# A causal mask copied into three score buffers by ScalarE, and a new order of maxima and feed-forward tiles, in a decoder layer

## The reference

```python
x = x + self_attention(layernorm(x))       # 16 query heads, 4 key heads of 16, latent projections, rotary, causal
x = x + cross_attention(layernorm(x), ctx) # 16 heads of 16, int mask shared by all batches and heads
x = x + ffn(layernorm(x))                  # 256 -> 1024 relu -> 256, hidden values and w2 rounded to 4-bit-exponent fp8

# both attentions
scores = q @ k.T * 16 ** -0.5
scores = where(masked, -inf or -1e9, scores)
out = softmax(scores) @ v
```

## Time and profile before

| what | value |
|---|---|
| median of 3 runs | 1891.46 us (1891.41 to 1894.48) |
| the profiled execution, its own time | 1879.75 us |
| its span, first to last instruction | 1878.1 us |
| mean granted TensorE clock | 0.962 |
| busy share of the span: TensorE / weight loads | 90% / 54% |
| busy share: VectorE / ScalarE / GpSimd | 66% / 59% / 37% |

### The profile page before, as it was taken

How to read it: one execution, slowest core, us unless ns; L and a number is a source line. 1 busy time by engine, 2 the same in 40 slices (tenths; PEclk the granted TensorE clock), 3 DMA queues, 4 the chain that set the end, 5 groups by cost and what they waited for, 6 DMA issues and landing times.

```text
span 1878.1 us, 34264 instructions
## 1 busy us (share of the span) xinstructions
PE 1683.7 (90%) x12302; PEld 1017.6 (54%) x12302; DVE 1242.5 (66%) x1908; ACT 1110.7 (59%) x1720; POOL 701.0 (37%) x962
## 2 busy tenths in 40 slices
PE   2879989899998989999899999989999898999887
PEld 1445555556554655655556554655655555565554
DVE  4467576676857667575776857668585766857562
ACT  3355665756567465656756566475656746565563
POOL 3260533625144261533526153262524426152300
PEclk7879999999999999999999998999999999999999
DMA  6351632725254270633626163271625427063310
GB/s 173 51 89 26 94 66 37 121 26 86 47 80 78 35 124 8 87 64 52 106 35 94 31 93 65 35 124 20 89 50 74 84 35 111 18 88 55 51 31 12
DMA packets 86607, 124.09 MB, mean 66 GB/s; under 512 B 10481, under 2 KB 53938, under 8 KB 86322
## 3 DMA queue, kind: packets, MB, share of 16 engines
q1 hardware_dynamic: 83650, 115.26, 40.5%
q0 software_dynamic: 2160, 7.87, 1.1%
q10 hardware_dynamic: 768, 0.57, 0.1%
HBM read 21.42 MB, written 8.39 MB: 16 GB/s over the span
## 4 chain that ended last, share of the span: by engine, by line
PE 62%; POOL 9%; issue 9%; ACT 7%; DMA 7%; DVE 6%; SPq 1%; POOLq 0%; ACTq 0%
PE o_pair L1312 12%; PE small L1398 7%; PE score L1273 6%; PE small L1429 5%; PE small L1143 4%; DMA Q<-q2p 3%; PE small L1325 3%; DVE negmax L894 3%; PE score L1250 3%; DMA Q<-negT 2%; PE score L1231 2%; PE score L1196 2%; PE small L1159 2%; POOL x L494 2%; POOL q1f L518 2%
## 5 line engine op out<-in xcount | busy, mean ns | idle before, releaser
L689 ACT ACTIVATE P<-score 128x1024 f32<-128x1024 f32 x448 | 448.4, 1025 | 145.5 <-PE score L1250 56.6
L894 DVE TENSOR_REDUCE negmax<-score 128x4 f32<-128x1024 f32 (+1 forms) x384 | 463.3, 1221 | 66.4 <-PE score L1231 49.9
L916 DVE TENSOR_TENSOR P<-P,cross_bound 128x1024 f32<-128x1024 f32 x192 | 251.0, 1330 | 118.1 <-ACT P L689 118.1
L1312 PE MATMUL o_pair<-P,V 128*32 128x256 f32 (+1 forms) x4096 | 293.8, 374 | 0.3 <-DVE P L916 0.3
L465 POOL TENSOR_TENSOR negrest<-negmax,negparts 128x32 f32<-128x32 f32 x64 | 15.9, 248 | 629.9 <-ACT negparts L650 629.5
L735 ACT ACTIVATE score<-cross_q 128x1024 f32<-128x1024 bf16 x192 | 194.9, 1021 | 31.8 <-DVE negmax L894 31.1
L1429 PE MATMUL small<-xnT,w 128*128 128x256 f32 x720 | 185.2, 379 | 0.0
L1273 PE MATMUL score<-Q,K 99*128 99x256 bf16 x1024 | 168.1, 291 | 8.2 <-ACT P L689 4.3
L1312 PEld LDWEIGHTS o_pair<-P,V 128*32 128x32 f32 x4096 | 87.3, 109 | 142.7 <-issue 86.7
L1231 PE MATMUL score<-K,Q 96*128 96x256 bf16 x768 | 119.3, 279 | 40.1 <-ACT score L735 19.7
L1273 PEld LDWEIGHTS score<-Q,K 99*128 99x128 bf16 x1024 | 87.4, 102 | 112.4 <-issue 63.6
(11 more groups left out here) (181 smaller groups left out, 3142.1 us busy)
## 6 DMA issues: line engine op xcount, KB each, us to landing
Q<-q1p SPq DMA_DIRECT2D x96, 256.0 KB, 5.9
K<-k2p SPq DMA_DIRECT2D x96, 256.0 KB, 8.3
Q<-q2p SPq DMA_DIRECT2D x192, 128.0 KB, 4.5
x_in<-in_x SPq DMA_DIRECT2D x16, 512.0 KB, 5.6
ctxT<-in_ctx SPq DMA_DIRECT2D x16, 512.0 KB, 6.3
k2f<-q1f SPq DMA_DIRECT2D x32, 256.0 KB, 4.9
out_y<-x POOLq DMA_DIRECT2D x15, 512.0 KB, 6.1
K<-k1p SPq DMA_DIRECT2D x96, 64.0 KB, 4.5
```

The source lines that it names most:

```text
L689: A.activation(P[:, t % 4, :], score[b][:, :, :], ACT.Exp, scale=SCALE).then_inc(score_free[b], 1)
L894: V.tensor_reduce(negmax[:, k, h:h + 1024 // w], s.rearrange("p (h w) -> p h w", w=w), AX.X, ALU.max, negate=True).then_inc(score_free[b], 1)
L916: V.tensor_tensor(p, p, cross_bound[:, t % 2, :].unsqueeze(1).broadcast_to([128, 4, SEQ]), ALU.min).then_inc(probs_masked[1], 1)
L1312: last = T.matmul(o_ps[ob][32 * j:32 * j + 32, SEQ * gg + q0:SEQ * gg + SEQ], v, p, start=s == 0, stop=end, tile_position=(0, 32 * j), ski ...
```

## The change

The self score tiles 3 to 11 get their causal mask from ScalarE (`self_premask`), as the cross tiles do, and no longer from TensorE; the self tiles use three buffers, with `o_pair` as the third, instead of two. Cross tile 8 is masked by TensorE instead of ScalarE. The cuts of the maxima are moved: GpSimd cuts the second cross half ahead of `add_ffn`, and the second self half is cut by ScalarE and GpSimd ahead of the exponentials instead of between them; `turn_max` moves from after tile 2 to after tile 1 (self) and tile 3 (cross). `add_bias2` moves to the next body. `h1` and `h2` go into the middle, ahead of and behind the transposes `xnT2_1`, the quarters of `h3` to `h7` are spread by `PIECES`, and VectorE makes the third part of the first cross query half before it applies the norm. `v2_0` is computed on both sides of self tile 2, and banks are given out in the new order.

```diff
 def body_users
-    attention = (["k2_0"] + p("m2T_1", "o2t0", "o2t1", "o2t2", "o2t3")
-                 + ["v2_0", "k2_1", "m1T_0"] + p("oT2_0", "oT2_1") + p("out2_0", "out2_1")
+    attention = (["k2_0"] + p("m2T_1", "o2t0", "o2t1", "o2t2") + ["v2_0"] + p("o2t3")
+                 + ["k2_1", "m1T_0"] + p("oT2_0", "oT2_1") + p("out2_0", "out2_1")
...
-              + ["xnT2_1"] + p("h1") + ["q2_1"])
-    scores = p("h2", "h3", "h4", "h5", "h6", "h7") + ["m2T_0"] + p("ffn0", "ffn1")
+              + p("h1") + ["xnT2_1"] + p("h2") + ["q2_1"])
+    scores = p("h3", "h4", "h5", "h6", "h7") + ["m2T_0"] + p("ffn0", "ffn1")
...
-        PE_MASKED = (2,)
+        PE_MASKED = (2, 8)
+        SELF_PE_MASKED = 3
+        PIECES = (2, 2, 1, 2, 2, 2, 2, 2, 1, 2, 2, 0)
+        EVICT_AFTER = (4, 6, 8, 11, 12)
...
 gpsimd, add_bias1
+                    pool.wait_ge(part3["q2"], GB * (g - 1) + 1)
 gpsimd, body
-                if prev:
-                    cut_rest(1, i - 1, 1)
-                    cut_third(1, i - 1, 1)
                 cut_rest(0, i, 0)
                 cut_third(0, i, 0)
                 if nxt:
                     inverse_root(0, i + 1)
+                if prev:
+                    add_bias2(i - 1)
                 cut_rest(0, i, 1)
+                cut_third(0, i, 1)
                 for t in range(N1):
...
-                    if t == 0:
-                        cut_third(0, i, 1)
...
-                add_bias2(i)
...
                     third("k1", i + 1)
+                cut_rest(1, i, 1)
+                cut_third(1, i, 1)
                 if prev:
                     add_ffn(st, i - 1)
 scalar, exponentials
-                    if t == 0:
+                    if t == 0 and a == 1:
                         cut_second(a, g, 1)
...
-                    if t == 2:
+                    if t == (1, 3)[a]:
                         maxima(st, a, 1)
 scalar
+            def self_premask(g, t):
+                n, before = self_tile(g, t)
+                act.wait_ge(score_free[n], before)
+                if t % 6 < 4:
+                    A.activation(bufs[n][:, :, :].rearrange("p c (j k) -> p (c j) k", j=2),
+                                 causal_q[:, :].unsqueeze(1).broadcast_to([128, 4, SEQ]),
+                                 ACT.Copy).then_inc(masked[n], 1)
...
 scalar, body
+                for t in range(3, 7):
+                    self_premask(i, t)
+                keys_second(st, 0)
+                self_premask(i, 7)
+                self_premask(i, 8)
                 cut_first(0, i, 0)
+                self_premask(i, 9)
                 cut_second(0, i, 0)
                 keys(st, 1)
-                keys_second(st, 0)
+                self_premask(i, 10)
                 maxima(st, 0, 0)
+                self_premask(i, 11)
+                keys_second(st, 1)
                 if prev:
                     turns(st, "oT2_", inT)
-                keys_second(st, 1)
                 cut_first(0, i, 1)
+                cut_second(0, i, 1)
                 exponentials(st, 0, i)
...
                 premask(i, 0)
+                if prev:
+                    hidden(st, [1])
                 turn_batch(st, "xnT2_1", 1, inT)
                 premask(i, 1)
                 if prev:
-                    hidden(st, [1])
+                    hidden(st, [2])
 vector, body
                 query2_rest(st, i, 0)
+                query2_third(i, 0)
                 norm_apply(1, x2, GB * i + 1, range(2, 4))
-                query2_third(i, 0)
                 query2_rest(st, i, 1)
 tensor, self_scores
+                    if not by_pe:
+                        pe.wait_ge(masked[n], use + 1)
+                    elif n == 2:
+                        for ob in range(2):
+                            if positive(g * UNITS):
+                                pe.wait_ge(o_free[ob], g * UNITS)
...
-                        for c in range(2):
-                            last = T.matmul(score[n][:, c, :], identb[:, :],
-                                            again(causal_q, 4), start=False, stop=True,
-                                            skip_group_check=True)
 tensor, attend
-                    if t == 2:
+                    if t == (1, 3)[a]:
                         turn_max(st, a, g, 1)
 tensor, body
                 if prev:
                     attend(st, 1, i - 1, "scores")
+                    tokens(st, "v2", ctxT, wv2, 0, 0)
...
+                tokens(st, "v2", ctxT, wv2, 0, 1)
                 self_scores(i, [3])
...
-                tokens(st, "v2", ctxT, wv2, 0, 0)
                 self_scores(i, [5])
-                tokens(st, "v2", ctxT, wv2, 0, 1)
                 self_scores(i, [6])
                 key2(st, 1, 0)
...
+                if prev:
+                    hidden(st, [1])
                 pe.wait_ge(xn_ready[1], GB * i + 2)
                 turned_batch(st, "xnT2_1", 1, xn)
                 if prev:
-                    hidden(st, [1])
+                    hidden(st, [2])
```

More of the change, by code:

```diff
@@ L303, in tile, with self_tile, cross_tile, masked_told @@
             return n % 2, g * (TILES // 2) + n // 2
-        def cross_use(g, t):
+        def self_tile(g, t):
+            n = t % 3
+            return n, g * (TILES // 2 if n < 2 else SELF_USES + CROSS_USES[2]) + t // 3
+        def cross_tile(g, t):
             n = CROSS_BUF[t]
-            return n, g * CROSS_USES[n] + CROSS_BUF[:t].count(n)
-        def cross_tile(g, t):
-            n, use = cross_use(g, t)
-            return (n, use) if n == 2 else (n, g * (TILES // 2) + N1 + CROSS_BUF[:t].count(n))
-        def cross_masked(g, t):
-            n = CROSS_BUF[t]
-            told = [u for u in range(N2) if u not in PE_MASKED and CROSS_BUF[u] == n]
-            return n, g * len(told) + told.index(t)
+            use = CROSS_BUF[:t].count(n)
+            return (n, g * (SELF_USES + CROSS_USES[2]) + SELF_USES + use) if n == 2 else \
+                (n, g * (TILES // 2) + SELF_USES + N1 // 2 + use)
+        def masked_told(n):
+            return ([("S1", t) for t in range(SELF_PE_MASKED, N1) if t % 3 == n]
+                    + [("S2", t) for t in range(N2) if t not in PE_MASKED and CROSS_BUF[t] == n])
+        def masked_use(phase, g, t):
+            n = t % 3 if phase == "S1" else CROSS_BUF[t]
+            told = masked_told(n)
+            return n, g * len(told) + told.index((phase, t))
         def last_cross_tiles(b):
@@ L600, in _ @@
             body(NG - 1, True, False)
-            cut_rest(1, NG - 1, 1)
-            cut_third(1, NG - 1, 1)
+            add_bias2(NG - 1)
             inverse_root(2, NG - 1)
@@ L645, in cut_first @@
                 last = N1 // GB * (b + 1) - 1
-                for t in (last, last - 1) if a == 0 else last_cross_tiles(b):
-                    n, before = tile("S1", g, t) if a == 0 else cross_tile(g, t)
+                for t in (last, last - 1, last - 2) if a == 0 else last_cross_tiles(b):
+                    n, before = self_tile(g, t) if a == 0 else cross_tile(g, t)
                     act.wait_ge(score_free[n], before + 1)
@@ L820, in body @@
                 for t in range(3, N2):
-                    premask(i, t)
-                    if prev and t in (3, 4, 6, 8, 10, 12):
-                        hidden(st, [max(t // 2 + 1, 2 + (t > 3))])
+                    if t not in PE_MASKED:
+                        premask(i, t)
+                    if prev and t in EVICT_AFTER:
+                        hidden(st, [3 + EVICT_AFTER.index(t)])
                     if t == 10:
@@ L1190, in self_scores @@
                     b, s = t // 6, t % 6
-                    n, before = tile("S1", g, t)
-                    if positive(before):
+                    n, before = self_tile(g, t)
+                    by_pe = t < SELF_PE_MASKED
+                    if not by_pe:
+                        _, use = masked_use("S1", g, t)
+                        pe.wait_ge(masked[n], use + 1)
[3 more added lines that the diff above has]
+                                pe.wait_ge(o_free[ob], g * UNITS)
+                    elif positive(before):
                         pe.wait_ge(score_free[n], before)
@@ L1219, in cross_scores @@
                     b = k // 2
-                    n, use = cross_masked(g, t) if t not in PE_MASKED else cross_tile(g, t)
+                    n, use = masked_use("S2", g, t) if t not in PE_MASKED else cross_tile(g, t)
                     if t not in PE_MASKED:
@@ L1560, in body @@
                     if prev and t < 12:
-                        for n in (2 * t, 2 * t + 1):
-                            hidden_part(st, 2 + n // 4, n % 4)
+                        for n in range(sum(PIECES[:t]), sum(PIECES[:t + 1])):
+                            hidden_part(st, 3 + n // 4, n % 4)
                     elif prev:
```

56 lines of the change are left out of this document (33 added, 23 removed).

## The result

The kernel became slower: 1922.12 us as the median of four runs (1911.23 to 1933.39), against 1891.43 for the kernel before. The ratio is 1.0174 with a 95% interval of 1.0130 to 1.0218. The forecast of 1821 us and its range, 1778 to 1864, both missed, and on the wrong side.

A forecast was written before the change was run, and what follows sets the result against it. TensorE was taken to be near its bound (busy 103.5 of about 111.5 us an iteration). Terms -3.0 + 2.2 - 0.9 - 2.0 - 0.7 = -4.4 us, times 16 is -70, from 1891.5 to 1821 us; range 1778 to 1864.

The forecast's parts named there:

- head of the cross part: Start of the cross probabilities: cuts ahead of `add_ffn` remove TensorE's 2.60 us wait; -3.0 us an iteration.
- Self maxima: Self maxima stage: VectorE sets it, so moving masks off TensorE buys almost nothing and new waits cost +2.2 us.
- (c): Self maxima: `k2_1` waits for VectorE to read `v2_0` after maximum 5; TensorE stands from +5.7 to +7.95 before `key2`.
- (d): Self maxima: turns of `oT2` queue on ScalarE behind tile 11's copy and `keys_second`; `out2` starts at 15.75, against 13.6.
- (b): Self maxima: the loop of ScalarE copy, tile and maximum takes 2.9 against VectorE's 3.6 us, so at no cost.
- Self probabilities: Self probabilities: earlier cuts and no 0.58 us DMA wait; tile 6 starts at 6.8 instead of 7.75; -0.9 us.
- Middle and cross maxima: Middle and cross maxima: `h2` moves ahead of the cross scores, cross maxima take 23.2 against 25.5 us; -2.0 together.
- Clock: Whole iteration: the 2.60 us gap and its clock fall go, new gaps come; half of today's 1.4, -0.7 us.
- C: Rival, chance 0.09: clock falls in the self maxima, 13.6 us at half clock an iteration; 1919 us.
- A: Rival, chance 0.12: copies and the bank of `k2_1` cost nothing, VectorE has no gap, clock stays up; 1768 us.
- B: Rival, chance 0.20: the head's wait moves; cross tile 8 waits for its maxima in the DMA queue; 1845 us.
- D: Rival, chance 0.05: no change; self maxima lose all the rest gains, +6.6 instead of +2.2; 1891 us.

The follow-up runs named there:

- the moved kernel: Changed kernel with 30 tiny matmuls (60 TensorE instructions) ahead of the loop, nothing inside the loop different: 1867.59 us, ratio 0.9871.
- The head cuts alone: Kernel before with only GpSimd's cuts of the second cross half moved ahead of `add_ffn` and the cross `turn_max` after tile 3: 1833.51 us, ratio 0.9700.
- with (c) and (d) mended: Padded changed kernel with `v2_0` read earlier, maxima sent earlier, `query2_third` later, `oT2` turns earlier: 1839.56 us with ScalarE's copies, 1822.29 with TensorE's masks.
- before moved by 60: Kernel before with 60 TensorE instructions (tiny matmuls) ahead of everything: 1891.08 us, ratio 0.9996.
- before moved by 144: Kernel before with 72 tiny matmuls (144 instructions) ahead of everything: 1907.48 us, ratio 1.0086.
- before moved by 200: Kernel before with 100 tiny matmuls (200 instructions) ahead of everything: 1892.04 us, ratio 1.0001.
- the same with zeros: Changed kernel padded by 60, two more matmuls adding zeros to each of the nine self tiles that ScalarE masks: 1868.83 us, ratio 0.9882.
- the same with TensorE's masks: Changed kernel padded by 60, all 12 self tiles masked by TensorE, three buffers kept: 1845.76 us, ratio 0.9761.

## Why the prediction was wrong, step by step

**The step that failed** is one that the sum did not have. Under "head of the cross part" I priced the wait that goes, and took every instruction as there when TensorE comes to it. The loop's own instructions are work too, loaded by a queue of their own, and I never asked whether the edit would move the loop. The reload is worth 54 us (1922.12 against 1867.59), 3.9 in each of 14 passes of the loop. The two profiled executions are 62.8 us apart (1933.39 and 1870.58). Of that, 48.9 us are waits for issue, less 10.7 by which the wait for the maxima at the same place shrinks (14.5 to 3.8, the latter from the waits view after); and the half clock is 10.5 us an iteration against 6.2 (4.7 before), half of which is 2.15, 30 us in 14 passes. That makes 68, a little more than the whole.

The Trainium skill (Runtime: NRT & Kernel Launch, "Instruction fetch mechanics") says that TensorE's instructions are held in a FIFO of 2048, refilled in blocks of 16 KiB or 256 instructions, and that a taken branch to a target outside the current window of two such blocks stalls for a fetch. The packets of 16 KB and the waits at the loop head agree. The window of two blocks does not: the loop of the kernel before has 1657 instructions, over six blocks, and is not loaded again.

The sum would have missed without the reload too, as the terms below show. The six stages of the moved kernel by the windows view, as in the earlier trace rows:

```profile
918.03:943.13 25.10, 24.18 (x230) 11.72 (x231) 21.38 (x29) 18.03 (x22) 6.24 (x5) 1.00 0.41 71
943.13:961.00 17.87, 13.56 (x88) 8.86 (x85) 13.69 (x18) 12.77 (x18) 4.21 (x7) 0.81 0.00 1
961.00:964.56 3.56, 3.56 (x17) 3.05 (x17) 2.21 (x4) 0.46 (x2) 0.49 (x2) 1.00 0.00 0
964.56:982.84 18.28, 17.85 (x183) 8.28 (x182) 9.35 (x25) 14.36 (x18) 10.03 (x21) 1.00 0.71 87
982.84:1004.25 21.41, 21.41 (x96) 13.99 (x95) 8.37 (x25) 12.38 (x25) 4.26 (x6) 1.00 0.36 57
1004.25:1029.18 24.93, 22.07 (x146) 16.27 (x144) 21.31 (x19) 18.62 (x31) 20.77 (x20) 1.00 0.70 113
```

The clock falls at different places in different iterations, so I also compare one iteration at full clock with one at full clock: 919.36 to 1029.48 us in the kernel before (110.1 us), 587.33 to 696.24 us in the moved one (108.9).

**Head of the cross part: -3.0.** Nearly right. From tile 0 to the last `times_v` it is 27.6 before and 25.2 us after at full clock, -2.4. The head cuts alone gain 60 us (1893.14 to 1833.51), 3.7 an iteration with the clock, and `turn_max` has no wait. Tile 6 starts 7.9 us after tile 0, where I had 7.1 to 7.5. GpSimd's add meets the third minimum and not the second, and my 0.4 for it was too small: the minimum took 2.83 us, the add 3.11 instead of 2.12, and TensorE waits 0.92 us for the minimum. Here are the timelines of VectorE and GpSimd in the moved kernel.

```profile
922.47 2.83 DVE L953 TENSOR_TENSOR P<-P,cross_bound 128x1024 f32<-128x1024 f32 x1 [0.24 <-ACT P L702]
...
921.11 3.11 POOL L509 TENSOR_TENSOR x<-x,ffn 128x1024 f32<-128x1024 f32 x1
```

**Self maxima: +2.2.** Right at full clock: 15.6 against 13.5 us is +2.1. In the window above it is 17.87 against 13.60, +4.3, because the clock falls there (0.81 over the stage). The gap of (c) is 1.88 us with VectorE's reading of `v2_0` as its releaser, as walked; behind it `key2` and the next tiles run at half clock and hand VectorE its next tile 1.89 us late, where I had 0.3 and 0.4. The 0.59 and 0.90 us before tile 11 and `out2` are (d). My own sign of being wrong, a clock below 0.9 in this stage, came up.

**Step (b), copies at no cost.** Wrong: even with (c) and (d) mended they cost 17 us against TensorE's masks. The bound that mattered stood in my own text, that VectorE sets this stage. The 2.8 us that TensorE was freed of bought nothing.

**Self probabilities: -0.9.** 18.28 against 18.90 is -0.6, with the clock at 1.00 in both rows; about right.

**Middle and cross maxima: -2.0.** 21.41 and 24.93 against 21.06 and 25.50 is -0.2, and the clock is 1.00 in all four rows: beside the reload this is the term that failed most. The middle came as walked (no query wait). The cross maxima are 1.7 longer than my 23.2: a wait of 1.17 us for a mask copy before tile 4 and one of about 0.9 at the loop head, where the maxima of the first cross half stand behind a key part in SyncE's queue. The timeline of TensorE in the moved kernel has both:

```profile
1011.09 0.61 PE L1273 MATMUL score<-K,Q 96*128 96x256 bf16 x4 [1.17 <-ACT score L761]
...
1029.18 1.04 PE L1315 MATMUL score<-Q,K 99*128 99x256 bf16 x8 [0.91 <-DMA Q<-negT]
```

**Clock: -0.7.** Wrong in sign in the profiled executions, without the reload too: the half clock went from 4.7 to 6.2 us an iteration. The mean of the 13 iterations lies 1.5 us above one at full clock before (111.56 and 110.1) and 2.1 above it in the moved kernel (111.0 and 108.9), which is +0.6. The repeated runs show no such difference: their clocks have a median of 0.955 before and 0.958 in the moved kernel.

**Sum.** At full clock the moved kernel is 1.2 us an iteration faster where the terms without the clock added up to -3.7, and with the clock 0.5 where I had 4.4. The medians say more, 24.8 us or 1.5 an iteration; the profiled execution of before lay 0.6% under its median and that of the moved kernel 0.2% over, which makes most of the difference. So 1821 would have been 47 us off even with the loop in place, just outside the range (1864). The walk of the self maxima was right; it was the cross maxima (1.7 short), the clock (1.3) and the head (0.6) that fell short.

**The rivals.** C's number, 1919 us, is near the 1922 measured, by luck. Its clock does fall in the self maxima and costs some 2 us there each time, and more than its break-even of 10.2 us at half clock was measured (10.5), though not the 13.6 on which 1919 rests. But it is not what made the kernel slower: the same self maxima average 17.3 us in the moved kernel and 16.6 in the changed one, and the moved one is 54 us faster. A fell with (b), (c) and (d). B's place was wrong: tile 8 did not wait; a wait for maxima came back elsewhere, at the loop head, and is small. D's 1891 needed +6.6 in the self maxima, and they had +4.3 with the clock. None of them held the reload.

## What to carry to other kernels

Before pricing a wait that goes at an engine's loop head, look at what it covers: compare the instruction packets of the page with the number of iterations, and look for waits for issue at the jump back. After any edit that adds or removes instructions, check that line again; this kernel lost 3% to the place of its loop, and 60 idle instructions ahead of it gave that back. Here, taking work from an engine that didn't bind the stage earned nothing, and putting it on a queue that serves the one that does cost 17 us. Price a stage at full clock first, then ask what a new gap does to the clock behind it: the gap of (c) cost 0.3 us by itself and five times that with the clock.

## What the runs showed of the hardware

**A loop's place decides whether it stays loaded.** Counting the TensorE instructions that the trace records, in blocks of 256, the loop starts and ends at these places in its blocks:

| kernel | before the loop / in it | start, end in the block | instruction packets |
|---|---|---|---|
| before | 941 / 1657 | 173, 38 | 19 |
| before moved by 60 | 1001 / 1657 | 233, 98 | 19 |
| before moved by 144 | 1085 / 1657 | 61, 182 | 28 |
| before moved by 200 | 1141 / 1657 | 117, 238 | 136 |
| after | 914 / 1621 | 146, 231 | 135 |
| after moved by 60 | 974 / 1621 | 206, 35 | 18 |
| the same with zeros | 1008 / 1657 | 240, 105 | 19 |
| the same with TensorE's masks | 1008 / 1662 | 240, 110 | 19 |

Put the true block boundary between 146 and 173 of this count, and the loops that stay loaded touch 7 blocks, those that are loaded again touch 8; the one moved by 144, with a single reload in its profiled execution, is past the edge by some 10 to 40 instructions. That rule is argued from eight places, not shown, and the trace's count can miss what it doesn't record. That a packet holds a block of 256 fits the count: with the loop counted once the trace has 941 + 1657 + 2207 TensorE instructions in the kernel before, some 253 for each of 19 packets. What is shown is that shifts of 60 and of 200 ahead of one and the same loop differ, and that its length is not the cause: the longest loop of the table, 1662, stays loaded.

**The reload costs idle time and clock.** At the loop head it is 2.63 to 3.29 us of idle time in the rows shown, 3.7 at most in the changed kernel. Behind it the clock can fall: `key2` takes 3.62 us instead of 1.88 in one of the two iterations shown, and 1.88 in the other.

**Half clock in a stage that VectorE bounds.** It costs time even there: the self maxima of the moved kernel take 15.59 us at full clock and 17.80 at 0.81. Added matmuls of zeros took the half clock from 6.2 to 2.6 us an iteration, made the stage 16.64 us at full clock, and left the time the same within 0.1% (1867.59 and 1868.83). The Trainium skill (TensorE: Matmul & The Clock Gate, "What's actually happening") says that activity holds the clock up; the runs agree, and show that holding it up this way can cost what it gives.

**A VectorE minimum beside a GpSimd add.** In the kernel before the minimum took 2.63 us and the add 2.12; in the moved kernel, where the add meets another minimum, 2.83 and 3.11. The other minima take about 1.2.
